# Local attention: the sums of the exponentials move from ScalarE's accumulator to one VectorE reduction

## The chip, the core and the metric

The kernel runs on one core of a Trainium2 chip. The metric is the device time of one execution in microseconds (us). The engines are TensorE (PE in the rows; PEld is its weight load), VectorE (DVE), ScalarE (ACT), GpSimd (POOL) and SyncE (SP), which issues the DMAs. Each engine works through its own instructions in program order and waits at semaphores for the others.

## What is computed

The program is a chain of eight stages over 2048 tokens with 128 features. Two of them are the same local-attention stage, which is what the change touches. Each instance has two layers, and each layer does the following (cut to what matters):

```python
def _layer(x, wqkv, qs, ksc, wo, lg, lb, w1, b1, w2, b2):
    h = shift_token(x)
    q, k, v = jnp.split(h @ wqkv, 3, axis=-1)      # 8 heads of 64
    q = l2norm(q) * qs
    k = l2norm(k) * ksc
    q, k = rotary_xpos(q, k)
    o = local_attention(q, k, v)                   # window of 64 and the window before
    x = x + o @ wo
    h = (shift_token(x) normalized) * lg + lb
    a, g = jnp.split(h @ w1 + b1, 2, axis=-1)
    return x + (a * gelu(g)) @ w2 + b2
```

In `local_attention` the scores of 64 queries against 128 keys are masked, `attn = softmax(sim)`, and `out = attn @ v`. The softmax is the exponential of the scores less their row maximum, divided by the sum of these exponentials over the row. That sum is the subject here.

## The kernel before

`local_layers` builds one instance. It treats 32 items (two layers of 16 tiles, a tile being 128 tokens). All engines run a software pipeline over slots `n`: in one slot each engine does one step for several items, and later steps belong to earlier items. The order of the steps on an engine is written out by hand in a loop over the slots, and semaphores join the engines.

TensorE does in one slot, in this order: `project_qk` (L1503, queries and keys of item n into the PSUM banks QK), `lin` (L1609, half of the feed-forward), `turn_n2`, `project_v`, `turn_qk` (L1521), `out_rows`, `gate`, `put_mask`, `turn_probs` (L1550, eight transposes of the probabilities, which go into the banks QK too), `shift_tokens`, `turn_tokens` (L1491, transposes a coming tile), `scores` (L1538), `down` (L1621), `context` (L1565).

ScalarE does `exponents` (L1668), `squares` (L1677, from the banks QK), `keep_context`, `scale_n2`, `keep_qk`, `keep_values`, `gelu` (L1718), `keep_tokens` (L1725 and L1726, writes `hT`) and `keep_probs` (L1733, writes `pT`). The exponentials of one item are eight instructions, one for each head, of 128 rows by 128 columns. Each has its own scale and bias for every row and also adds up its results into one column of `den`.

VectorE does `row_max` (L1852 and L1854), `add_feed`, `norms`, `normalize_n2`, `gated` (L1888), `invert_sums` (L1897, the reciprocal of `den`), `rotate` (L1907 and L1908, two products from the banks QK), `add_rows`, `square_sums` (L1921) and `row_stats`. GpSimd multiplies the exponentials by the reciprocals in `normalize_probs` (L1765), and does the copies and sums around the rotated queries and keys.

The waits that matter for the steps around the change, besides those in the functions printed below:

```python
# turn_probs(k) on TensorE
pe.wait_ge(S["probs_ready"], k + 1)
if valid(k + 2):
    pe.wait_ge(S["rot_ready"], k + 3)
# down(e) on TensorE
pe.wait_ge(S["pT_ready"], e + 4)
# gated(e) on VectorE
dve.wait_ge(S["gelu_ready"], e + 1)
dve.wait_ge(S["lin_ps"], e + 1)
# rotate(m) on VectorE
dve.wait_ge(S["qksq_ready"], m + 1)
```

A call `link(...)` makes the next VectorE instruction wait until the one in it has completed.

Of the kernel before, what the change touches and what calls it, by code (L numbers as in the profile page):

```python
# [10 lines left out]
ALU = mybir.AluOpType  # L11
ACT = mybir.ActivationFunctionType
X_AXIS = mybir.AxisListType.X
# [39 lines left out]
def counted(eng, sem):  # L53

    count = [0]

    def link(ins):
        count[0] += 1
        ins.then_inc(sem, 1)
        eng.wait_ge(sem, count[0])  # L60

    return link
# [1344 lines left out]
def local_layers(nc, W, C, X, tag):  # L1407
# [17 lines left out]
    RN = 8  # L1425

    with ExitStack() as ctx:
        def sb(name, shape, dt=F32):
            return ctx.enter_context(nc.sbuf_tensor(f"{tag}_{name}", shape, dt))
# [14 lines left out]
        ss, rn, rtmp = sb("ss", [P, 17]), sb("rn", [P, RN, 17]), sb("rtmp", [P, 2, 17])  # L1444
        sm = sb("sm", [P, 2, H, P])
        nmx, nb = sb("nmx", [P, H]), sb("nb", [P, 2, H])
        den, rden = sb("den", [P, 2, H]), sb("rden", [P, 2, H])
# [25 lines left out]
        with nc.Block() as block:  # L1473
# [186 lines left out]
            def _(act):  # L1660
                def exponents(k):
                    act.wait_ge(S["max_ready"], k + 1)
                    if k >= 2:
                        act.wait_ge(S["pT_ps"], k - 1)
                    for part in range(2):
                        for i in range(PAIRS):
                            g, head = 4 * part + i, 2 * i + part
                            ins = act.activation(sm[:, k % 2, g, :], ps[:, SC + part, P * i:P * i + P], ACT.Exp,  # L1668
                                                 bias=nb[:, k % 2, g:g + 1], scale=rn[:, k % RN, head:head + 1],
                                                 accum_out=den[:, k % 2, g:g + 1])  # L1670
                    ins.then_inc(S["exp_ready"], 1)

                def squares(n):
# [65 lines left out]
                for n in SLOTS:  # L1739
                    if valid(n - 2):  # L1740
                        exponents(n - 2)
                    if valid(n):
                        squares(n)
                    if valid(n - 3):
                        keep_context(n - 3)
                    if valid(n - 4):
                        scale_n2(n - 4)
                    if valid(n - 1):
                        keep_qk(n - 1)
                    if valid(n):  # L1750
                        keep_values(n)
                    if valid(n - 4):
                        gelu(n - 4)
                    if valid(n + 3):
                        keep_tokens(n + 3)
                    if valid(n - 2):
                        keep_probs(n - 2)
# [86 lines left out]
            def _(dve):  # L1844
                link = counted(dve, S["dve_step"])
# [47 lines left out]
                def invert_sums(k):  # L1893
                    dve.wait_ge(S["exp_ready"], k + 1)
                    if k >= 2:
                        dve.wait_ge(S["probs_ready"], k - 1)
                    dve.reciprocal(rden[:, k % 2, :], den[:, k % 2, :]).then_inc(S["rden_ready"], 1)  # L1897

                def rotate(m):
# [61 lines left out]
                for n in SLOTS:  # L1961
                    if valid(n - 1):
                        row_max(n - 1)
                    if valid(n - 5):
                        add_feed(n - 5)
                    if valid(n) or valid(n - 3):
                        norms(n)
                    if valid(n - 3):
                        normalize_n2(n, n - 3)
                    if valid(n - 4):  # L1970
                        gated(n - 4)
                    if valid(n - 1):
                        invert_sums(n - 1)
                    if valid(n + 1):
                        rotate(n + 1)
                    if n == 0:
                        dve.wait_ge(S["tab_rest"], 16)
                        link(scale_first_tables(tab[:, 0, EARLY:TILES]))
                    if valid(n - 2):
                        add_rows(n - 2)  # L1980
                    if valid(n + 1):
                        square_sums(n + 1)
                    if valid(n - 2):
                        row_stats(n - 2)
# [586 lines left out]
```

## Time and profile before

| | |
|---|---|
| median of 3 runs | 4412.28 us (4410.9 to 4415.93) |
| the profiled execution | 4411.24 us |
| its span, first to last instruction | 4409.4 us |
| TensorE busy | 3583.9 us (81%) |
| VectorE busy | 2945.4 us (67%) |
| ScalarE busy | 1853.5 us (42%) |
| GpSimd busy | 1521.7 us (35%) |
| exponentials of the two local stages (L1668), 512 | 226.3 us busy, 463 ns each |

The busy shares are averages over eight stages with different limits. The two local stages lie at about 2000 to 2410 us and 3975 to 4409 us of the span. In a row of the timeline the first number is the start in us from the span's beginning, the second the duration of the row; several like instructions in a row are merged, with their number behind the x. In square brackets stands the idle time of the engine just before, and what ended it.

### The profile page before, as it was taken

What the parts mean: (1) busy time and instruction counts of PE and PEld (TensorE: products, weight loads), DVE (VectorE), ACT (ScalarE), POOL (GpSimd) and SP (SyncE); (2) the same over time, 40 slices, a digit from 0 to 9 for tenths busy, and PEclk for the clock granted to TensorE, in tenths of its full rate; (3) what the DMA queues carried; (4) which work ended last, traced back from release to release, by engine and by line L of the source; (5) the groups of instructions that cost most, each with busy time, mean ns of one, the idle gap of its engine ahead of it and who ended that gap; (6) DMA issues with size and microseconds to landing.
All of it is one profiled execution on the core that took longest, in us unless ns stands there. A gap on an engine that the chain in (4) does not pass through costs nothing. (4 is left out here: it accounts for less than half of the span.)

```text
span 4409.4 us, 61231 instructions
## 1 busy us (share of the span) xinstructions
PE 3583.9 (81%) x22279; PEld 2171.7 (49%) x22279; DVE 2945.4 (67%) x5904; ACT 1853.5 (42%) x3362; POOL 1521.7 (35%) x980
## 2 busy tenths in 40 slices
PE   4888888888883554227998499999999999997997
PEld 3667666676672122215777233333333333334776
DVE  3675666666754776566777577766766766657776
ACT  2334333333340000115998133333333333346997
POOL 0110110111100000004665065565655556565664
PEclk9999999999996555568999699999999999998999
DMA  2000000000001000000000100000000000000000
GB/s 82 1 1 1 1 1 1 1 1 1 1 1 45 0 0 0 6 0 39 2 2 2 33 1 1 1 1 1 1 1 1 1 1 1 1 1 39 2 2 11
DMA packets 21617, 31.28 MB, mean 7 GB/s; under 512 B 8818, under 2 KB 18460, under 8 KB 20252
## 3 DMA queue, kind: packets, MB, share of 16 engines
q1 hardware_dynamic: 21340, 27.46, 2.0%
q8 instruction: 189, 3.10, 0.3%
q14 instruction: 88, 0.72, 0.1%
HBM read 26.40 MB, written 1.05 MB: 6 GB/s over the span
## 5 line engine op out<-in xcount | busy, mean ns | idle before, releaser
L2291 POOL TENSOR_TENSOR global_acc_pool<-global_acc_pool,global_probs 128x1024 f32<-128x1024 f32 x320 | 776.0, 2425 | 471.1 <-ACT global_probs L2244 454.3
L2339 DVE TENSOR_REDUCE global_part<-global_ps 128x2 f32<-128x1024 f32 x512 | 624.5, 1220 | 429.9 <-PE global_ps L2099 429.8
L2244 ACT ACTIVATE global_probs<-global_ps 128x1024 f32<-128x1024 f32 x512 | 524.3, 1024 | 883.3 <-PE global_ps L2117 818.3
L2117 PE MATMUL global_ps<-global_q,global_k 64*128 64x512 f32 x2048 | 522.5, 588 | 0.0
L2128 PE MATMUL global_ps<-global_probs,global_v 128*64 128x512 f32 x2048 | 495.7, 605 | 0.0
L2099 PE MATMUL global_ps<-global_khh,global_qhh 64*128 64x512 f32 x1024 | 324.8, 631 | 35.6 <-DVE global_part L2339 33.5
L2115 PE MATMUL global_ps<-global_mrow,global_first 64*128 64x512 f32 x1024 | 323.8, 629 | 0.0
L554 DVE COPY_PREDICATED delta_Y<-delta_tri,delta_ps 128x512 f32<-128x512 uint32 x192 | 139.1, 728 | 269.7 <-PE delta_ps L304 268.3
L527 POOL TENSOR_TENSOR delta_state<-delta_state,delta_eg 128x1024 f32<-128x1024 f32 x16 | 34.3, 2145 | 705.1 <-PE delta_ps L318 705.1
L2128 PEld LDWEIGHTS global_ps<-global_probs,global_v 128*64 128x64 f32 x2048 | 124.2, 136 | 282.6 <-issue 161.5
L2099 PEld LDWEIGHTS global_ps<-global_khh,global_qhh 64*128 64x128 f32 x1024 | 97.9, 188 | 322.6 <-DVE global_part L2339 259.0
L281 PE MATMUL delta_ps<-delta_wconv,delta_x1T 128*128 128x512 f32 x512 | 247.3, 635 | 0.0
L2117 PEld LDWEIGHTS global_ps<-global_q,global_k 64*128 64x128 f32 x2048 | 194.0, 186 | 86.1 <-issue 61.2
L1668 ACT ACTIVATE local_sm<-local_ps,local_nb,local_rn 128x128 f32<-128x128 f32 x512 | 226.3, 463 | 15.9 <-DVE local_nb L1854 14.5
L442 ACT ACTIVATE delta_T<-delta_ps 128x512 f32<-128x512 f32 x192 | 114.7, 597 | 227.7 <-PE delta_ps L288 227.5
L2291 DVE TENSOR_TENSOR global_acc<-global_acc,global_probs 128x1024 f32<-128x1024 f32 x128 | 194.6, 1520 | 10.1 <-ACT global_probs L2244 10.1
L296 PE MATMUL delta_ps<-delta_T,delta_NT 128*128 128x128 f32 x1536 | 199.5, 286 | 0.0
L296 PEld LDWEIGHTS delta_ps<-delta_T,delta_NT 128*128 128x128 f32 x1536 | 190.7, 201 | 9.3 <-issue 7.2
L304 PE MATMUL delta_ps<-delta_Y,delta_NTp 128*128 128x128 f32 x1536 | 193.6, 279 | 0.0
L304 PEld LDWEIGHTS delta_ps<-delta_Y,delta_NTp 128*128 128x128 f32 x1536 | 180.7, 192 | 0.0
L288 PE MATMUL delta_ps<-C_tile,delta_Y 128*128 128x128 f32 x768 | 129.6, 294 | 60.0 <-DVE delta_Y L625 40.6
L2115 PEld LDWEIGHTS global_ps<-global_mrow,global_first 64*128 64x128 f32 x1024 | 96.4, 185 | 163.4 <-issue 151.9
(590 smaller groups left out, 7268.8 us busy)
## 6 DMA issues: line engine op xcount, KB each, us to landing
delta_cw<-in_L_attn_a_conv_w SPq DMA_DIRECT2D x1, 4096.0 KB, 12.1
local_tab<-in_rot_tables SPq DMA_DIRECT2D x2, 2048.0 KB, 11.9
local_tab<-in_rot_tables SPq DMA_DIRECT2D x2, 1536.0 KB, 7.4
localw_wqkv<-in_L_ffn_wqkv SPq DMA_DIRECT2D x2, 768.0 KB
delta_wqkvz<-in_L_attn_a_W_qkvz SPq DMA_DIRECT2D x1, 1024.0 KB, 14.2
local_tab<-in_rot_tables SPq DMA_DIRECT2D x2, 512.0 KB, 4.0
global_cos<-in_rope_cos SPq DMA_DIRECT2D x2, 512.0 KB, 10.6
global_sin<-in_rope_sin SPq DMA_DIRECT2D x2, 512.0 KB, 12.2
```

What stands on the lines that cost most here:

```text
L281: mm = pe.matmul(banks(bank), x1T[:, j:j + P], wconv[:, j, column:column + 512], start=(j == 0), stop=(j == TAPS - 1))
L296: mm = pe.matmul(bank_heads(0, 2)[:, h, :], NT[:, h, :], T[:, h, :], start=True, stop=True)
L304: mm = pe.matmul(bank_heads(2, 2)[:, h, :], NTp[:, h, :], Y[:, new, h, :], start=True, stop=True)
L554: dve.copy_predicated(Y[:, new, half(s), :], over_middle(tri[:, l, :], 4), bank_heads(2 + s, 1)).then_inc(S["Y_ready"], 1)
L1668: ins = act.activation(sm[:, k % 2, g, :], ps[:, SC + part, P * i:P * i + P], ACT.Exp, bias=nb[:, k % 2, g:g + 1], scale=rn[:, k % RN, hea ...
L2099: mm = pe.matmul(ps[:, 5 + s, :], qhh[own, u % 2, P * qt:P * qt + P], khh[own, group_of(u) % 2, BLK * c:BLK * c + BLK], start=True, stop=True)
L2115: pe.matmul(ps[:, 2 * (at % 2) + s, :], first[own, :], mrow[own, u % 2, :], start=True, stop=False)
L2117: mm = pe.matmul(ps[:, 2 * (at % 2) + s, :], k2[own, group_of(u) % 2, P * k:P * k + P], q[own, u % 3, :], start=False, stop=True)
L2128: mm = pe.matmul(ps[own, 4, :], v[:, k, HD * g:HD * g + HD], probs[:, at % RING, BLK * s:BLK * s + BLK], start=(k == 0), stop=(k == TILES ...
L2244: act.activation(probs[:, at % RING, :], ps[:, 2 * (at % 2):2 * (at % 2) + 2, :].rearrange("p b n -> p (b n)"), ACT.Exp).then_inc(S["probs ...
L2291: ins = eng.tensor_tensor(sums[:, u % 2, :], sums[:, u % 2, :], probs[:, at % RING, :], ALU.add)
L2339: dve.tensor_reduce(part[:, u % 2, r % SLOTS, :], ps[:, 5:7, :], X_AXIS, ALU.max)\
```

## The change

The eight exponentials of an item no longer add up their results. Instead `invert_sums`, which runs on VectorE, first reduces the whole tile of exponentials (128 rows, 8 heads of 128 columns) to the eight sums, and then takes the reciprocal as before.

```diff
                             ins = act.activation(sm[:, k % 2, g, :], ps[:, SC + part, P * i:P * i + P], ACT.Exp,
-                                                 bias=nb[:, k % 2, g:g + 1], scale=rn[:, k % RN, head:head + 1],
-                                                 accum_out=den[:, k % 2, g:g + 1])
+                                                 bias=nb[:, k % 2, g:g + 1], scale=rn[:, k % RN, head:head + 1])
                     ins.then_inc(S["exp_ready"], 1)
...
                     dve.wait_ge(S["exp_ready"], k + 1)
                     if k >= 2:
                         dve.wait_ge(S["probs_ready"], k - 1)
+                    link(dve.tensor_reduce(den[:, k % 2, :], sm[:, k % 2], X_AXIS, ALU.add))
                     dve.reciprocal(rden[:, k % 2, :], den[:, k % 2, :]).then_inc(S["rden_ready"], 1)
```

On VectorE, one slot of the regular stretch reads like this before the change, from `normalize_n2` to `square_sums`:

```order
L1878 TENSOR_SCALAR local_n<-local_ps,local_mv,local_rn 128x64
L1888 SCALAR_TENSOR_TENSOR local_hg<-local_ps,localw_b,local_ge 128x128 x2
L1888 SCALAR_TENSOR_TENSOR local_hg<-local_ps,localw_b,local_ge 85x128
L1897 RECIPROCAL local_rden<-local_den 128x8
L1907 TENSOR_TENSOR local_rc<-local_ps,local_tab 128x1024
L1908 TENSOR_TENSOR local_rs<-local_ps,local_tab 128x1024
L1917 TENSOR_TENSOR local_x<-local_ps,local_xl 128x128
L1921 TENSOR_REDUCE local_ss<-local_qksq 128x16
```

The same place in the changed kernel, where the lines between L1669 and L1895 are numbered one lower:

```order
L1877 TENSOR_SCALAR local_n<-local_ps,local_mv,local_rn 128x64
L1887 SCALAR_TENSOR_TENSOR local_hg<-local_ps,localw_b,local_ge 128x128 x2
L1887 SCALAR_TENSOR_TENSOR local_hg<-local_ps,localw_b,local_ge 85x128
L1896 TENSOR_REDUCE local_den<-local_sm 128x8
L1897 RECIPROCAL local_rden<-local_den 128x8
L1907 TENSOR_TENSOR local_rc<-local_ps,local_tab 128x1024
L1908 TENSOR_TENSOR local_rs<-local_ps,local_tab 128x1024
L1917 TENSOR_TENSOR local_x<-local_ps,local_xl 128x128
L1921 TENSOR_REDUCE local_ss<-local_qksq 128x16
```

One row is new, the reduction of `local_sm` to `local_den`; it stands after `gated` and ahead of the reciprocal and `rotate`. No other VectorE row has moved.

On ScalarE the same slot reads, before the change, from `gelu` to the squares of the next slot:

```order
L1718 ACTIVATE local_ge<-local_ps,localw_b 85x128
L1725 ACTIVATE local_hT<-local_ps 64x128
L1726 ACTIVATE local_hT<-local_ps 64x128
L1733 ACTIVATE local_pT<-local_ps 128x1024
L1668 ACT_TABLE_LOAD
L1668 ACTIVATE local_sm,local_den<-local_ps,local_nb,local_rn 128x128 x8
L1677 ACTIVATE local_qksq<-local_ps 128x1024
```

In the changed kernel the eight exponentials write `local_sm` alone, and all rows stand in the same order:

```order
L1717 ACTIVATE local_ge<-local_ps,localw_b 85x128
L1724 ACTIVATE local_hT<-local_ps 64x128
L1725 ACTIVATE local_hT<-local_ps 64x128
L1732 ACTIVATE local_pT<-local_ps 128x1024
L1668 ACT_TABLE_LOAD
L1668 ACTIVATE local_sm<-local_ps,local_nb,local_rn 128x128 x8
L1676 ACTIVATE local_qksq<-local_ps 128x1024
```

## Rows read from the trace of the kernel before

**Rows 1.** Busy us (instructions) by engine in each local stage's regular stretch

```profile
core 0: us, PE busy (x) PEld busy (x) DVE busy (x) ACT busy (x) POOL busy (x), PEclk, DMA share, GB/s
2068.42:2352.50 284.08, 262.39 (x2872) 208.52 (x2872) 223.45 (x647) 281.76 (x721) 181.84 (x187) 1.00 0.01 2
4054.38:4338.36 283.98, 262.74 (x2877) 209.38 (x2877) 223.50 (x648) 281.67 (x719) 181.47 (x187) 1.00 0.01 2
```

**Rows 2.** Timeline, VectorE: the row maximum at both ends of that stretch

```profile
2068.42 1.22 DVE L1852 TENSOR_REDUCE local_nmx<-local_ps 128x8 f32<-128x1024 f32 x1 [0.69 <-PE local_ps L1538]
...
2352.50 1.23 DVE L1852 TENSOR_REDUCE local_nmx<-local_ps 128x8 f32<-128x1024 f32 x1 [0.69 <-PE local_ps L1538]
```

**Rows 3.** Timeline, TensorE, in one slot of the second local stage

```profile
4187.15 1.98 PE L1503 MATMUL local_ps<-localw_wqkv,local_hT 128*128 128x512 f32 x4
4188.97 0.83 PE L1609 MATMUL local_ps<-local_nT,localw_w 128*128 128x128 f32 x6
...
4193.60 1.03 PE L1550 MATMUL local_ps<-C_tile,local_sm 128*128 128x128 f32 x8
...
4194.87 0.28 PE L1491 MATMUL local_ps<-C_tile,local_xl 128*128 128x128 f32 x1
...
4197.07 0.91 PE L1621 MATMUL local_ps<-localw_w,local_hg 128*128 128x128 f32 x6 [0.88 <-ACT local_pT L1733]
```

**Rows 4.** Timeline, ScalarE, in the same slot

```profile
4189.45 0.48 ACT L1668 ACTIVATE local_sm<-local_ps,local_nb,local_rn 128x128 f32<-128x128 f32 x1
4189.80 0.23 ACT L1668 ACTIVATION_READ_ACCUMULATOR local_sm<-local_ps,local_nb,local_rn 128x1 f32 x1
4189.89 1.05 ACT L1677 ACTIVATE local_qksq<-local_ps 128x1024 f32<-128x1024 f32 x1
...
4194.56 0.87 ACT L1718 ACTIVATE local_ge<-local_ps,localw_b 128x128 f32<-128x128 f32 x3
4195.32 0.26 ACT L1725 ACTIVATE local_hT<-local_ps 64x128 f32<-64x128 f32 x1
...
4195.90 1.02 ACT L1733 ACTIVATE local_pT<-local_ps 128x1024 f32<-128x1024 f32 x1
```

**Rows 5.** Timeline, VectorE, in the same slot

```profile
4189.90 0.86 DVE L1888 SCALAR_TENSOR_TENSOR local_hg<-local_ps,localw_b,local_ge 128x128 f32<-128x128 f32 x3 [0.83 <-issue]
4190.68 0.19 DVE L1897 RECIPROCAL local_rden<-local_den 128x8 f32<-128x8 f32 x1
4190.97 1.23 DVE L1907 TENSOR_TENSOR local_rc<-local_ps,local_tab 128x1024 f32<-128x1024 f32 x1
4192.11 1.22 DVE L1908 TENSOR_TENSOR local_rs<-local_ps,local_tab 128x1024 f32<-128x1024 f32 x1
...
4196.42 1.23 DVE L1852 TENSOR_REDUCE local_nmx<-local_ps 128x8 f32<-128x1024 f32 x1 [0.69 <-PE local_ps L1538]
4197.68 0.17 DVE L1854 TENSOR_TENSOR local_nb<-local_nmx,local_rn 128x8 f32<-128x8 f32 x1
```

**Rows 6.** Timeline, all engines, in an early slot of the first local stage

```profile
2052.95 1.22 DVE L1908 TENSOR_TENSOR local_rs<-local_ps,local_tab 128x1024 f32<-128x1024 f32 x1
...
2054.31 1.06 PE L1550 MATMUL local_ps<-C_tile,local_sm 128*128 128x128 f32 x8 [0.30 <-DVE local_rs L1908]
...
2055.38 0.28 PE L1491 MATMUL local_ps<-C_tile,local_xl 128*128 128x128 f32 x1
...
2055.70 0.27 ACT L1725 ACTIVATE local_hT<-local_ps 64x128 f32<-64x128 f32 x1 [1.98 <-PE local_ps L1491]
```

**Rows 7.** Timeline, VectorE, in another slot of the first stage

```profile
2110.34 0.18 DVE L1897 RECIPROCAL local_rden<-local_den 128x8 f32<-128x8 f32 x1
2110.45 1.17 DVE L1907 TENSOR_TENSOR local_rc<-local_ps,local_tab 128x1024 f32<-128x1024 f32 x1
```

**Rows 8.** Groups by line: busy us, mean ns of one, idle before

```profile
L1921 DVE TENSOR_REDUCE local_ss<-local_qksq 128x16 f32<-128x1024 f32 x64 | 77.4, 1209 | 0.1
```

**Rows 9.** Timeline, GpSimd, in the slot of rows 3 to 5

```profile
4190.95 1.90 POOL L1765 TENSOR_TENSOR local_sm<-local_sm,local_rden 128x1024 f32<-128x1024 f32 x1 [0.82 <-DVE local_rden L1897]
```

**Rows 10.** Busy us by engine in a stretch of the first stage

```profile
900.00:1000.00 100.00, 87.73 (x569) 71.67 (x569) 59.61 (x146) 39.77 (x64) 10.53 (x4) 0.97 0.00 1
```

## The prediction

> **What bounds the kernel now.** I read the busy shares of the two local-attention stages first. Both instances have a long regular stretch, and in it ScalarE (ACT) is busy 281.76 of 284.08 us, TensorE 262.39 (92%), VectorE 223.45 (79%), GpSimd 181.84 (64%) [rows 1]. VectorE's row-maximum reduction starts at 2068.42 and 2352.50 with 23 more of its kind between, so a slot (one tile of 128 tokens) takes 284.08 / 24 = 11.84 us [rows 2]. The second instance gives the same figure, 283.98 / 24 = 11.83 [rows 1]. At first sight ACT is the bound and VectorE has 2.5 us of room in every slot.
>
> Occupancy does not say what a change on VectorE costs, so I next followed one slot around its hand-offs, at 4187 to 4199.5 us. The work of one slot runs in a ring, because each engine executes in program order and the PSUM banks QK and the tile `hT` are reused. The ring begins at `turn_probs`, the eight TensorE transposes of the probabilities (L1550). Its links are these:
>
> 1. `turn_probs` starts at 4193.60; TensorE then shifts, transposes the next tokens (L1491, ends 4194.87 + 0.28 = 4195.15) [rows 3].
> 2. ACT copies these to `hT` from 4195.32, then copies the probabilities to `pT` from 4195.90 for 1.02 us [rows 4].
> 3. TensorE waits 0.88 us for `pT` and starts `down` (L1621) at 4197.07 [rows 3]. From `turn_probs` to `down`: 3.47 us.
> 4. TensorE does `down`, `context`, `project_qk`, `lin` without a wait. One slot earlier `down` began at 4197.07 - 11.84 = 4185.23, `project_qk` at 4187.15 and `lin` (L1609) at 4188.97 [rows 3]. VectorE's `gated` (L1888) needs `lin`'s result and starts at 4189.90, after an idle time of 0.83 us [rows 5]. It starts 0.10 after `lin` ends (4188.97 + 0.83), and nothing else that it waits for is as late. From `down` to `gated`: 4.67 us.
> 5. VectorE does `gated`, the reciprocal of the sums (L1897, 0.78 later, 4190.68), then the two products of `rotate`, at 4190.97 and 4192.11, the second for 1.22 us: they end at 4193.33 [rows 5]. `turn_probs` writes the PSUM banks that `rotate` reads, so it waits for that end. This closes the ring.
>
> The ring therefore nearly fills the slot: it holds only three small gaps. After `rotate` ends, TensorE needs 0.14 us at most: in an early slot, where it really waited for VectorE, `rotate` ended at 2052.95 + 1.22 = 2054.17 and `turn_probs` started at 2054.31 [rows 6]. Here it started 0.27 after. That leaves **0.13**. A reciprocal can be followed by `rotate` in 0.11 us (2110.34 to 2110.45) [rows 7]; here it took 0.29, since `rotate` also waits for ACT's squares, which end at 4189.89 + 1.05 = 4190.94 [rows 4]. That leaves **0.18**. ACT can start `hT` 0.04 after the transpose ends (2055.38 + 0.28 to 2055.70) [rows 6]; here it took 0.17, as ACT was in `gelu` until 4195.43 [rows 4]. That leaves **0.13**. In all 0.44 us of slack in 11.84.
>
> **The change, part by part.** ACT loses eight accumulator reads per slot. A read starts 0.35 us after its exponential and the next instruction 0.09 us after the read (4189.45, 4189.80, 4189.89) [rows 4]. If the read's start is where the next instruction could begin, each one saves 0.09 us, so 8 x 0.09 = 0.72 us per slot. Upper bound: `gelu`, also 128 wide but with one pointer operand, issues its three in 0.87 us, so at most 0.29 apiece, against 0.35 + 0.09 = 0.44 for an exponential with its read [rows 4]; that is 8 x 0.15 = 1.2 us. Lower bound nothing. I take 0.72. None of the exponentials lies on the ring above: their only exit into it is through the squares and through the sums, both of which have waited on VectorE's side only for 0.18 us. So the saving on ACT buys at most the closing of gaps.
>
> The Trainium skill (ScalarE: Activation LUTs, What ACT_TABLE_LOAD costs) would price such an ACTIVATE with two pointer operands at 186 + 2 x 93 + 0.833 x 128 = 465 ns less 93 of overlap, an estimate of 0.37 us, so a saving of 0.06 us each and 0.5 us per slot; this case's 0.48 us for one ACTIVATE agrees with the first figure, and the sum below is the same either way.
>
> VectorE gains one reduction of 128x1024 to 128x8 in SBUF per slot. The same shape stands in `square_sums` (L1921, 128x1024 f32 from SBUF to 128x16), 1209 ns mean over 64 [rows 8]. The new one is linked: the reciprocal waits for its completion, as L1854 waits for L1852, which is a 1.23 us reduction with 1.26 us from start to start (4196.42 to 4197.68) [rows 5]. From these: at least 1.21, at most 1.26; I take 1.26. It is placed between `gated` and the reciprocal, so it sits in link 5 of the ring. Nothing in that link can pass it: `rotate` is queued behind it on VectorE, and `turn_probs`, then every later TensorE step of the slot, waits for `rotate`.
>
> GpSimd's normalization, which waits for the reciprocal, is late by the same amount. It starts 0.27 after the reciprocal and takes 1.90 [rows 5, 9], together 2.17, while `rotate` with its hand-off takes 0.11 + 1.14 + 1.22 + 0.14 = 2.61. So it stays hidden behind `rotate` by about 0.3 to 0.4 us.
>
> The new ring is 11.84 + 1.26 - 0.44 = **12.66 us**, against 11.84: **+0.82 us per slot**. Summed by links it is 3.34 + 4.67 + 0.78 + 1.26 + 0.11 + 2.36 + 0.14 = 12.66. All engines have less than that to do (TensorE 262.39 / 24 = 10.93, VectorE 9.31 + 1.21 = 10.5, ACT 11.74 - 0.72 = 11.0 [rows 1]), so the ring is the bound.
>
> Over 24 slots in each of two stages: 48 x 0.82 = 39 us. Each stage has seven more slots, at its start and end. There the exponentials do stand in line with the sums and the rest, so one pays 1.26 - 0.72 = 0.54 at most; where `rotate` waits for the squares that follow the exponentials (1.05 us [rows 4]), the reduction lies beside them and costs less than the exponentials save. I take 0.25 as the middle between 0 and 0.54: 14 x 0.25 = 3.5 us. Sum: +43 us. The profiled execution took 4411.24 us, 1.04 below the median of the three runs. 4411.2 + 43 = 4454.
>
> **The rivals.**
> *Faster: ACT's relief decides (chance 0.08).* ACT is 99% busy [rows 1], and if the reduction falls into VectorE's 0.83 us wait before `gated` and the 0.69 before the maximum, the slot follows ACT, down by 0.72 to 11.12: 48 x -0.72 = -35 us, 4377. TensorE's 10.93 still fits. For it speaks ACT's busy share alone; against it, the reduction stands behind `gated` and `gated`'s wait is for TensorE, so the wait cannot be filled. It would decide if the slack of link 5 were over 1.26 us; I find 0.31 there. The Trainium skill (Perfetto Trace Analysis, Identifying the Most-Contended Engine) says that the engine of the highest occupancy should be relieved first, which is what this rival follows; rows here show the occupancy, not that it decides.
> *No change (0.05).* The ring has more slack than I see, about 1.2 us, for example because the hand-off gaps are longer by waits that the trace does not name. The ring then lands near ACT's old pace: 4404 to 4420.
> *No slack recovered (0.10).* The three gaps turn out to be minimum hand-offs and stay: 1.26 in full, 48 x 1.26 + 7 = +67, 4478.
> *The clock gives way (0.05).* TensorE's busy share falls from 92% to 10.93 / 12.66 = 86%. In a stretch of the first stage with 87.7% the granted clock is 0.97, not 1.00 as here [rows 1, 10]. Some 3% of the time at 1.2 instead of 2.4 GHz lengthens the 7 us of TensorE work that lie in the ring by 0.2: +10 us more, 4464.
> *The ring as computed (0.72).* Its own range: the gaps recover between 0.26 and 0.6 us, so +0.66 to +1.0 per slot, 32 to 48 us, with 0 to 7 us for the other slots: 4443 to 4466.
>
> **Range and chances.** The likeliest case gives 4454. The range takes in the whole of it, the clock and most of the unrecovered slack, and leaves out the two cases at or below 4420: 4438 to 4480, holding about 8 in 10. A difference under 0.2% (about 9 us) can't be told from no change here. Faster 0.08, same 0.05, slower 0.87.
>
> **What would show it.** In the profile after, the L1852 starts should stand 12.5 to 12.8 us apart. The new reduction should take 1.21 us. TensorE should show a wait of about 0.9 us before L1550, released by VectorE's `rotate` (L1908), which it does not have now. ACT's share should fall to about 11.0 / 12.66 = 87% and some of its idle time should stand before `hT`. `gated` should still start 0.10 after `lin`. If L1550 has no wait, or its releaser is GpSimd's normalization, link 5 or the GpSimd step is wrong; if the slot is shorter than 11.84, the ring is not the bound at all. The sum would also be wrong if reading tiles that ACT has just written made the reduction longer than 1.26, or if `down` came to wait for something else than `pT`.

## The result, and the profile after

The changed kernel takes 4453.05 us (median of four runs, 4451.59 to 4456.84), the kernel before 4411.59 beside it: a ratio of 1.0096, with a 95% interval of 1.0082 to 1.0109. It is slower by 41.5 us, which is 1 us from the forecast. The profiled execution took 4451.59 us with a span of 4449.8, 40.4 more than before.

Busy time in the regular stretch of both local stages. The 24 slots of such a stretch now take 303.29 and 303.45 us:

```profile
core 0: us, PE busy (x) PEld busy (x) DVE busy (x) ACT busy (x) POOL busy (x), PEclk, DMA share, GB/s
2080.05:2383.34 303.29, 264.92 (x2879) 207.17 (x2880) 250.45 (x673) 270.23 (x528) 181.34 (x187) 1.00 0.01 2
4073.84:4377.29 303.45, 265.14 (x2879) 207.17 (x2880) 251.01 (x673) 270.22 (x528) 181.32 (x187) 1.00 0.01 2
```

This answers to [rows 1]. A slot takes 303.29 / 24 = 12.64 us where it took 11.84 (12.66 was forecast). ScalarE (ACT) has fallen from 99% to 89% busy, and no engine is near full: this is what a stretch looks like that waits in a ring. The two stretches are 303.29 - 284.08 = 19.21 and 303.45 - 283.98 = 19.47 us longer, together 38.7 of the 40.4 us.

One slot on TensorE, to be held against [rows 3]:

```profile
4229.76 0.83 PE L1609 MATMUL local_ps<-local_nT,localw_w 128*128 128x128 f32 x6
...
4233.74 0.71 PE L1529 MATMUL local_ps<-local_mask,local_identr 128*128 128x512 f32 x2
4235.32 1.07 PE L1550 MATMUL local_ps<-C_tile,local_sm 128*128 128x128 f32 x8 [0.87 <-DVE local_rs L1908]
...
4236.62 0.28 PE L1491 MATMUL local_ps<-C_tile,local_xl 128*128 128x128 f32 x1
...
4238.68 0.91 PE L1621 MATMUL local_ps<-localw_w,local_hg 128*128 128x128 f32 x6 [0.75 <-ACT local_pT L1732]
...
4242.42 0.83 PE L1609 MATMUL local_ps<-local_nT,localw_w 128*128 128x128 f32 x6
```

The reader should look at the square bracket behind L1550. TensorE now waits 0.87 us there, for VectorE's second `rotate` product. The idle time begins where the row before, `put_mask` (L1529), ends. From `turn_probs` to `down` it is 4238.68 - 4235.32 = 3.36 us (3.47 before, 3.34 forecast), since ScalarE now starts `hT` as soon as the transposes end. The same slot on VectorE, for [rows 5]:

```profile
4230.69 0.86 DVE L1887 SCALAR_TENSOR_TENSOR local_hg<-local_ps,localw_b,local_ge 128x128 f32<-128x128 f32 x3 [0.84 <-issue]
4231.47 1.20 DVE L1896 TENSOR_REDUCE local_den<-local_sm 128x8 f32<-128x1024 f32 x1
4232.71 0.20 DVE L1897 RECIPROCAL local_rden<-local_den 128x8 f32<-128x8 f32 x1
4232.83 1.21 DVE L1907 TENSOR_TENSOR local_rc<-local_ps,local_tab 128x1024 f32<-128x1024 f32 x1
4233.96 1.22 DVE L1908 TENSOR_TENSOR local_rs<-local_ps,local_tab 128x1024 f32<-128x1024 f32 x1
...
4238.17 1.23 DVE L1851 TENSOR_REDUCE local_nmx<-local_ps 128x8 f32<-128x1024 f32 x1 [0.69 <-PE local_ps L1538]
```

`gated` (now L1887) still starts 0.93 after `lin` (4229.76). The reduction follows 0.78 later, the reciprocal 1.24 after that, `rotate` 0.12 after the reciprocal, and it ends at 4233.96 + 1.22 = 4235.18, from which `turn_probs` starts 0.14 later. Every link has the length that the sum gave it within 0.03 us. On ScalarE, for [rows 4], and GpSimd, for [rows 9]:

```profile
4232.46 0.60 ACT L1699 ACTIVATE local_qT<-local_ps 128x512 f32<-128x512 f32 x1 [0.61 <-PE local_ps L1521]
...
4236.93 0.27 ACT L1724 ACTIVATE local_hT<-local_ps 64x128 f32<-64x128 f32 x1 [0.71 <-PE local_ps L1491]
...
4237.51 1.02 ACT L1732 ACTIVATE local_pT<-local_ps 128x1024 f32<-128x1024 f32 x1
...
4239.85 2.90 ACT L1668 ACTIVATE local_sm<-local_ps,local_nb,local_rn 128x128 f32<-128x128 f32 x8
4242.62 1.05 ACT L1676 ACTIVATE local_qksq<-local_ps 128x1024 f32<-128x1024 f32 x1
```

```profile
4232.99 1.90 POOL L1764 TENSOR_TENSOR local_sm<-local_sm,local_rden 128x1024 f32<-128x1024 f32 x1 [2.08 <-DVE local_rden L1897]
```

The eight exponentials now take 4242.62 - 4239.85 = 2.77 us, where those of before, with their reads, took 3.50 (4198.23 to 4201.73 in its trace): ScalarE got 0.73 us, and spends it in the waits for TensorE before `qT` (0.61) and `hT` (0.71). GpSimd's normalization ends at 4234.89, 0.29 ahead of `rotate`, so it stays hidden. That it is close shows in the list of waits, where the transposes' weight loads (PEld) are put down to GpSimd and the transposes themselves to VectorE (us in total, times, longest):

```profile
PEld local_ps L1550 <- POOL local_sm L1764: 25.0, 20, 1.4
PE local_ps L1550 <- DVE local_rs L1908: 16.9, 20, 1.0
```

Two rows of the groups by line, the new reduction and the one from which its price was taken [rows 8]:

```profile
L1921 DVE TENSOR_REDUCE local_ss<-local_qksq 128x16 f32<-128x1024 f32 x64 | 77.3, 1208 | 0.1
L1896 DVE TENSOR_REDUCE local_den<-local_sm 128x8 f32<-128x1024 f32 x64 | 77.2, 1206 | 3.7 <-ACT local_sm L1668 3.7
```

### The profile page after: what moved, and what is told of

Its sections match the earlier page's. It is cut to its first block and busy times, and to the rows that moved or that the text cites. A ratio compares the mean times of both kernels' runs of the same rounds, so it can differ in the third digit from the quotient of the medians.

```text
span 4449.8 us, 60783 instructions
## 1 busy us (share of the span) xinstructions
PE 3592.2 (81%) x22279; PEld 2169.1 (49%) x22279; DVE 3017.5 (68%) x5968; ACT 1820.4 (41%) x2850; POOL 1521.7 (34%) x980
## 5 line engine op out<-in xcount | busy, mean ns | idle before, releaser
L1668 ACT ACTIVATE local_sm<-local_ps,local_nb,local_rn 128x128 f32<-128x128 f32 x512 | 186.0, 469 | 20.5 <-DVE local_nb L1853 19.6
L288 PE MATMUL delta_ps<-C_tile,delta_Y 128*128 128x128 f32 x768 | 129.6, 294 | 59.8 <-DVE delta_Y L625 40.4
```

## The experiments

A slot's length is everywhere the distance between the starts of VectorE's row maximum in the regular stretch.

**ScalarE's relief alone.** Against the changed kernel, the reduction is left out, and `den` is filled once with a constant, so the kernel no longer computes the sums:

```diff
+                pool.memset(den[:], 64.0)
...
-                    link(dve.tensor_reduce(den[:, k % 2, :], sm[:, k % 2], X_AXIS, ALU.add))
```

> The eight accumulations are gone and no reduction takes their place: the sums are left out of the computation (the reciprocal is taken of a constant), so this times ScalarE's relief alone. Ring theory: the ring without the reduction is 11.84 - 0.44 = 11.40 us a slot, longer than ScalarE's 11.1, so -0.44 x 48 = -21 us and some -3 for the other slots: 4388. Rival, occupancy: the slot follows ScalarE down by its full 0.72 us, -35 us and more at the ends: 4370. Second rival: another chain through ScalarE's copies holds 11.8 us whatever the exponentials take: 4405 or above.

It took 4404.32 us, ratio 0.9985 (0.9975 to 0.9995): 7 us less than before, and a slot stayed at exactly 11.84, so none of it came from the regular stretch. Neither the ring of 11.40 nor ScalarE's load held it. ScalarE was busy 266.54 of 283.90 us, 94%. The trace has what did:

```profile
4230.69 1.04 PE L1521 MATMUL local_ps<-C_tile,local_qkr 128*128 128x128 f32 x8
...
4237.16 0.91 PE L1621 MATMUL local_ps<-localw_w,local_hg 128*128 128x128 f32 x6 [0.99 <-ACT local_pT L1732]
...
4242.53 0.71 PE L1521 MATMUL local_ps<-C_tile,local_qkr 128*128 128x128 f32 x5
```

```profile
4231.77 0.60 ACT L1699 ACTIVATE local_qT<-local_ps 128x512 f32<-128x512 f32 x1 [0.63 <-PE local_ps L1521]
4232.26 0.59 ACT L1701 ACTIVATE local_kT<-local_ps 128x512 f32<-128x512 f32 x1
4232.74 0.61 ACT L1709 ACTIVATE local_v<-local_ps 128x512 f32<-128x512 f32 x1
4233.36 1.28 ACT L1717 ACT_TABLE_LOAD   x1
4234.66 0.87 ACT L1717 ACTIVATE local_ge<-local_ps,localw_b 128x128 f32<-128x128 f32 x3
4235.42 0.26 ACT L1724 ACTIVATE local_hT<-local_ps 64x128 f32<-64x128 f32 x1
...
4235.99 1.02 ACT L1732 ACTIVATE local_pT<-local_ps 128x1024 f32<-128x1024 f32 x1
```

TensorE's `turn_qk` (L1521) ends at 4231.73. ScalarE waited 0.63 us for it, then runs without a pause through `qT`, `kT`, the values, the table load, `gelu`, `hT` and `pT`; `down` starts at 4237.16, 0.15 after `pT` ends, and TensorE comes without a pause to the next `turn_qk`, which starts 11.84 after the last. This is a second ring. Any chain that closes in a steady pipeline measures one slot; what marks this one is that it holds no idle time beyond the hand-offs, where the first ring still has its 0.44. In the kernel before it is as tight:

```profile
4190.60 1.04 PE L1521 MATMUL local_ps<-C_tile,local_qkr 128*128 128x128 f32 x8
4191.27 0.51 ACT L1693 ACTIVATE local_nT<-local_ps,localw_lb,localw_lg 128x128 f32<-128x128 f32 x1
4191.67 0.60 ACT L1700 ACTIVATE local_qT<-local_ps 128x512 f32<-128x512 f32 x1
```

`turn_qk` ends there at 4191.64, and `qT` starts 0.03 later. No bracket shows a wait, because ScalarE's eight accumulations (0.73 us) filled the idle time, so that ScalarE looked full. My second rival was right here, the ring theory's number was not.

**The reduction alone.** Against the kernel before, the accumulations stay and feed the result, and VectorE reduces into a tile of its own:

```diff
+                    link(dve.tensor_reduce(den2[:, k % 2, :], sm[:, k % 2], X_AXIS, ALU.add))
                     dve.reciprocal(rden[:, k % 2, :], den[:, k % 2, :]).then_inc(S["rden_ready"], 1)
```

> The accumulations stay and feed the result as in the kernel before; VectorE does the reduction too, at the place of the change, into a tile that nobody reads. This times the reduction alone. Ring theory: ScalarE has 11.74 us to do in a ring of 12.65, so its relief is worth nothing in the 48 regular slots; they stay at 12.65 and only the slots at the ends lose: 4456 to 4464. Rival: the relief on ScalarE gave part of the cost back in every slot; then a slot is longer than 12.65 by up to 0.72 us and the time is 4470 to 4490.

It took 4457.71 us, ratio 1.0104 (1.0087 to 1.0120), and a slot 12.63 to 12.67 us, as in the changed kernel. In the regular stretch ScalarE's relief is thus worth nothing once the reduction is there; the 4 to 5 us between the two kernels are not in these slots.

**Another place.** Against the changed kernel:

```diff
+                    if valid(n - 1):
+                        invert_sums(n - 1)
                     if valid(n - 4):
                         gated(n - 4)
-                    if valid(n - 1):
-                        invert_sums(n - 1)
```

> The changed kernel with reduction and reciprocal moved ahead of gated, where VectorE idles 0.84 us for TensorE. Ring theory: gated is then late by what the reduction exceeds the idle time. From turn_probs: probabilities copied at 3.21, table load and exponentials end at 7.30, reduction from 7.45, reciprocal 8.7, gated 8.8, rotate 9.6, its end 11.94, next turn_probs 12.1. So 12.1 us a slot, +0.26 x 48 + 2 = +14 us against the kernel before: 4426. Rival: the reduction costs its 1.2 us wherever it stands on VectorE: 4453 as the changed kernel.

It took 4425.18 us, ratio 1.0031 (1.0021 to 1.0042), a slot of 12.10. Two thirds of the loss are gone with the same instructions on the same engine. VectorE's rows say where the limit is now:

```profile
4258.49 1.22 DVE L1896 TENSOR_REDUCE local_den<-local_sm 128x8 f32<-128x1024 f32 x1 [0.27 <-ACT local_sm L1668]
4259.75 0.20 DVE L1897 RECIPROCAL local_rden<-local_den 128x8 f32<-128x8 f32 x1
4259.87 0.86 DVE L1887 SCALAR_TENSOR_TENSOR local_hg<-local_ps,localw_b,local_ge 128x128 f32<-128x128 f32 x3
4260.65 1.21 DVE L1907 TENSOR_TENSOR local_rc<-local_ps,local_tab 128x1024 f32<-128x1024 f32 x1
4261.78 1.21 DVE L1908 TENSOR_TENSOR local_rs<-local_ps,local_tab 128x1024 f32<-128x1024 f32 x1
```

The bracket behind the reduction names ScalarE's exponentials, 0.27 us; `gated` follows the reciprocal at once, where it had waited for `lin`.

**Half the dose.** Heads 0 to 3 (in the order in which `sm` holds them) are reduced on VectorE, heads 4 to 7 accumulate. The reduction stands once behind `gated` and once ahead of it. Against the changed kernel:

```diff
+                def sum_early(k):
+                    dve.wait_ge(S["exp_half"], k + 1)
+                    link(dve.tensor_reduce(den[:, k % 2, 0:4], sm[:, k % 2, 0:4], X_AXIS, ALU.add))
...
-                    link(dve.tensor_reduce(den[:, k % 2, :], sm[:, k % 2], X_AXIS, ALU.add))
```

and on ScalarE the last four exponentials have their `accum_out` again, and the fourth signals `exp_half`. Behind `gated`:

> Heads 0 to 3 are summed by VectorE in one reduction of 512 columns behind gated, at the place of the change; heads 4 to 7 accumulate on ScalarE as before. Ring theory: a linked reduction half as long takes about 0.53 + 0.17 = 0.70 us, so the ring is 11.40 + 0.70 = 12.10, +0.26 x 48 + 1 = +14 us: 4425. Rival, half the work costs half of the measured loss: +20 us: 4432. Rival, ScalarE decides with its relief of 0.36 us: -17 us: 4394.

It took 4424.48 us, ratio 1.0027 (1.0016 to 1.0038), a slot of 12.10 to 12.13, as the ring gives. From the reduction's start to the reciprocal:

```profile
4225.07 0.67 DVE L1897 TENSOR_REDUCE local_den<-local_sm 128x4 f32<-128x512 f32 x1
4225.78 0.20 DVE L1903 RECIPROCAL local_rden<-local_den 128x8 f32<-128x8 f32 x1
```

So two doses are measured: 12.64 - 1.24 = 11.40 and, with the mean slot of 12.12, 12.12 - 0.71 = 11.41. Both leave the ring without a reduction at the 11.40 us that the slack of 0.44 had given. With `sum_early` called ahead of `gated` instead:

> Heads 0 to 3 are summed by VectorE in one reduction of 512 columns ahead of gated, in its idle time, as soon as their exponentials are there; heads 4 to 7 accumulate as before. Two-ring theory: the VectorE ring then holds no reduction (11.40 us) and ScalarE has 0.36 us less, but the run without sums stayed at 11.84 us a slot with ScalarE idle 0.63 us before qT, so a second ring (turn_qk, qT, kT, v, table load, gelu, hT, pT, down, project_qk, turn_qk) holds 11.84. So the slot stays at 11.84 and the time is 4402 to 4412. Rival, ScalarE's load decides: 11.48 us a slot, -17 us, 4394 or less.

It took 4405.56 us, ratio 0.9984 (0.9975 to 0.9993), a slot of 11.85: the reduction costs nothing there, and the second ring stands.

**The second ring shortened.** ScalarE copies the values while it would wait for `turn_qk`:

```diff
+                    if valid(n):
+                        keep_values(n)
                     if valid(n - 1):
                         keep_qk(n - 1)
-                    if valid(n):
-                        keep_values(n)
```

With heads 0 to 3 reduced ahead of `gated`, alone on the kernel before, and on the kernel without sums:

> As the run with heads 0 to 3 summed ahead of gated, and ScalarE copies the values (keep_values) ahead of the queries and keys (keep_qk), which takes 0.48 us out of the second ring. Two-ring theory: second ring 11.36, VectorE ring 11.40, ScalarE's own load 11.74 - 0.36 = 11.38 and 0.1 of gaps: 11.4 to 11.5 us a slot, -0.35 to -0.44 x 48 = -17 to -21 and -3 at the ends: 4388 to 4392. Rival: there is no such second ring, and moving the copy changes nothing against the run without it: 4402 to 4412.

> The kernel before with keep_values ahead of keep_qk alone. Two-ring theory: ScalarE has no idle time in which to put the copy (281.76 of 284.08 us busy), so its load of 11.74 and the gaps keep the slot at 11.75 to 11.84: 4407 to 4412. Rival: the second ring alone held the slot; then it falls by 0.44 to 11.40 and the time to 4390.

> No accumulations and no reduction (the sums are left out of the computation), with keep_values ahead of keep_qk. It tests the first ring's length without the reduction, 11.40 us, which the other run without sums could not show behind the second ring. Two-ring theory: the slot is 11.40, 48 x -0.44 = -21 us against the other run without sums (4404): 4383. Rival: the slot is held at 11.84 by something else: 4404.

| kernel | us | ratio (95%) | slot, us |
|---|---|---|---|
| half ahead, values first | 4393.74 | 0.9956 (0.9943 to 0.9970) | 11.60 |
| values first alone | 4418.21 | 1.0015 (1.0006 to 1.0024) | 11.96 |
| no sums, values first | 4386.58 | 0.9941 (0.9927 to 0.9954) | 11.61 |

The second ring is real: the same swap gives 12 us (with half the sums, against 4405.56) and 18 us (without sums, against 4404.32; 48 x 0.23 = 11 of them in the regular slots) where ScalarE has time to spare. But 11.40 to 11.50 was expected, and two kernels with different loads on ScalarE and VectorE both stop at 11.6. TensorE's rows of the first of them:

```profile
4151.66 0.91 PE L1621 MATMUL local_ps<-localw_w,local_hg 128*128 128x128 f32 x6 [0.75 <-ACT local_pT L1735]
...
4159.93 1.03 PE L1550 MATMUL local_ps<-C_tile,local_sm 128*128 128x128 f32 x8
...
4163.26 0.91 PE L1621 MATMUL local_ps<-localw_w,local_hg 128*128 128x128 f32 x6 [0.75 <-ACT local_pT L1735]
```

TensorE needs 4159.93 - 4151.66 = 8.27 us from `down` to `turn_probs`, with no wait for another engine in it, and 3.33 from there to `down` by way of `hT` (which starts 0.03 after the transposes end) and `pT`: a third ring of 11.60. On the kernel before the swap cost 0.12 us a slot, which I had not expected. There ScalarE has no spare time, the copy only makes `kT` later, and `put_mask` waits for it (16 times 0.2 us):

```profile
PEld local_ps L1529 <- ACT local_kT L1702: 3.4, 16, 0.2
```

and with it `turn_probs` and the transposes for `hT`. In its slot at 4160 us these end at 4161.26, and `hT` starts at 4161.30, 0.89 after `gelu` started (4160.41), where it took 0.76 in the kernel before [rows 4]. So the later transposes now hold ScalarE by 0.13, and TensorE's way from `down` to `turn_probs` is 8.63 us long (4151.09 to 4159.72): the third ring, made longer. The size fits the 0.12 us; no run takes it apart.

**The third ring shortened.** In the kernel with half the sums ahead and the values first, TensorE transposes the coming tile ahead of `shift_tokens`; on top of that, five heads in place of four are then reduced on VectorE:

```diff
+                    if valid(n + 3):
+                        turn_tokens(n + 3)
                     if valid(n - 3):
                         shift_tokens(n - 3)
-                    if valid(n + 3):
-                        turn_tokens(n + 3)
```

> The run with heads 0 to 3 summed ahead of gated and the values first, and TensorE transposes the coming tile (turn_tokens) ahead of shift_tokens. Third-ring theory: two different kernels both stopped at 11.61 us a slot, which is TensorE's own run from down to turn_probs (8.27) plus turn_probs to down by way of hT and pT (3.34). The transposes 0.35 to 0.4 us earlier shorten this to 11.25; then ScalarE's load of 11.49 a slot decides: -0.12 x 48 = -6 us against the run before it, 4386 to 4390. Rival: 11.61 has another cause and nothing changes: 4394.

> As e11_tokens_first, with five heads summed by VectorE ahead of gated and three accumulated, so ScalarE has 0.09 us less in a slot: 11.40. The reduction of 640 columns (about 0.83 us linked) still ends before lin does. Third-ring theory: ScalarE's load decides, 11.40 to 11.45 us a slot, a further -2 to -4 us: 4383 to 4386. Rival: the reduction now holds gated back, or the VectorE ring of 11.40 with its hand-offs decides; then it is no faster than with four heads, 4388 or more.

They took 4387.12 us, ratio 0.9951 (0.9937 to 0.9965), and 4384.03 us, ratio 0.9938 (0.9924 to 0.9952), with slots of 11.46 and 11.39. The intervals of the two overlap, but the slots' lengths in the traces differ by 0.07 us, and so does ScalarE's busy time in a slot (11.36 and 11.29 us). The busy times of ten slots of the last one:

```profile
core 0: us, PE busy (x) PEld busy (x) DVE busy (x) ACT busy (x) POOL busy (x), PEclk, DMA share, GB/s
4142.52:4256.36 113.84, 108.20 (x1198) 87.32 (x1198) 98.23 (x280) 112.87 (x251) 73.59 (x75) 1.00 0.01 2
```

ScalarE is busy 112.87 of 113.84 us, 99% as in the kernel before, and this time the slot followed when load was taken from it, which it did not do in the run without sums. It may not follow much further: `qT` starts at 4172.03, again 0.03 after `turn_qk` ends (4170.96 + 1.04), so the second ring, shortened by the swap, stands right beside. This is the fastest version here: 27 us below the kernel before (and some 69 below the changed one), with part of the change's idea in it, at another place.

## Why the prediction was right

**The ring (right, by its links).** The prediction's sum 3.34 + 4.67 + 0.78 + 1.26 + 0.11 + 2.36 + 0.14 = 12.66 met 12.64. The largest difference is the reduction with its link, 1.24 in place of 1.26. That the reduction is the whole cause is shown by adding it alone (12.65 a slot); that its place is, by moving it (12.10); that it acts by its length, by half of it (12.11).

**The slack of 0.44 (right in sum).** The ring without a reduction is 11.40 by two doses. All three gaps closed: 0.14 after `rotate`, 0.12 after the reciprocal, and `hT` 0.03 after the transposes (4236.62 + 0.28 to 4236.93). The rival in which none closes is out.

**ScalarE's relief (size right, its value right, its reading incomplete).** 0.72 us a slot was forecast and 0.73 came. It was worth nothing in the regular slots. But the prediction took ScalarE at 99% for the bound of the kernel before, and expected 11.0 / 12.66 = 87% after; it was 89%, 11.26 us a slot. The 0.2 us are overlap that was lost: in the kernel before, `qT` starts 0.11 before its predecessor ends (4191.27 + 0.51 to 4191.67), and `hT` too (4194.56 + 0.87 to 4195.32); now both stand behind a wait. The run without sums shows that in the kernel before a second ring of 11.84 ran through ScalarE's copies beside its load, so that the "faster" rival could not have gained 0.72 a slot even with the reduction free: it would have gained nothing there and some 7 us elsewhere. The step that was wrong is thus that rival's price (4377 against a measured 4404), not the forecast. Occupancy, on which the Trainium skill's rule (Perfetto Trace Analysis, Identifying the Most-Contended Engine) rests, named ScalarE; taking its load down to 94% did not shorten a slot. The prediction's estimate of one exponential from the Trainium skill (ScalarE: Activation LUTs, What ACT_TABLE_LOAD costs) is added up wrongly: its terms give 479 ns, not 465, and 0.39 us after the overlap, not 0.37. The traces have 463 to 469 ns on the mean and 0.35 us from start to start, and the sum did not use the estimate.

**GpSimd (right).** Hidden with 0.29 us to spare, 0.3 to 0.4 forecast.

**The other slots.** 3.5 us were put on them, and 40.4 - 38.7 = 1.7 is all that the two profiled executions have left for them and for the rest of the program; no run splits it. From one profiled execution to the other the change is thus 40.4 us where 43 were forecast, so that the medians meet the forecast within 1 us is partly luck.

**The clock (right).** The granted clock stayed at 1.00 in the stretch although TensorE's share fell to 264.92 / 303.29 = 87%. In that rival's working, a mean clock of 0.97 between 2.4 and 1.2 GHz means 6% of the time at the lower level, not 3%; its 0.2 us for 7 us of work is what 0.97 gives.

## What to carry to other kernels

When an engine is 99% busy, still look for rings: follow one period from hand-off to hand-off until it closes, and add up the links. The price of an instruction put on a half-idle engine is what it adds to the longest ring less the gaps in it, and the same instruction ahead of the waiting one, in its idle time, may cost nothing. Taking load from a full engine gains nothing while a ring of the same length stands beside it.

## What the runs showed of the hardware

An accumulating exponential of 128x128 with its read costs 0.09 us more than a plain one in sequence (3.50 against 2.77 us for eight), though the read is listed with 210 ns: reads overlap with the exponential before and the instruction after. A linked VectorE reduction from SBUF took 672 ns for 512 columns, 811 for 640 and 1206 for 1024, that is about 1.04 ns a column and 0.14 us fixed, an estimate from these three. In the change it takes 1.24 us from its start to the reciprocal's and takes 0.73 from ScalarE, so the exchange loses even in the sum over both engines.
